# Joining the last 512 rows of a mixture of experts on VectorE, expert by expert, in place of identity products on TensorE

## The chip, the cores and the metric

The kernel runs on one core of one Trainium2 chip. The metric is the device time of one execution in microseconds (us). Three runs of the kernel before gave 262.27, 261.35 and 261.16 us; the median is 261.35 us.

## The reference, cut to what matters

A small language tower over 8 sequences of 256 tokens (2048 rows of 64 channels): a causal convolution tower with log-softmax, a linear attention block, a softmax attention block, and at the end a mixture of 8 experts, top 2 of them weighted. What the change touches is the end of the last stage:

```python
out = zeros_like(flat)                                  # flat: 2048 x 64
for e in range(8):
    hh = silu(flat @ w1[e].T) * (flat @ w3[e].T)        # 2048 x 170
    out = out + weights[:, e:e + 1] * (hh @ w2[e].T)    # 2048 x 64
h = h + x + out
```

Every row needs the sum over the 8 experts of its 64 down-projected values times that row's gate of that expert, plus the row that went in (`hx`, the sum of the residuals).

## The kernel before, in words

The program is written engine by engine, with counting semaphores set and awaited; nothing plans the order, it is the order of the code. Rows lie in 16 tiles of 128 (one row per partition); the last stage takes them in four groups of 512 rows (`PAIRS` = 4, four tiles each). The 170 hidden values of each of the 8 experts make 11 units of up to 128 per group (8 main parts, three packed remainders; `ORDER` says in which order), so the stage has 44 units, u = 0 to 43.

One unit goes through the engines like this: TensorE makes the two up projections into two PSUM banks; ScalarE applies silu (line 746); VectorE multiplies silu by the other projection (line 1229, `hh`); ScalarE rounds the product to float16 (line 731, semaphore `hi_ready`); GpSimd subtracts to get the float16 remainder (`low_part`, line 407, semaphore `lo_ready`). When the parts of a pair of experts k (experts 2k and 2k+1) are there, TensorE makes the down projections of the four tiles (`down(n_, k, t_)`, line 1699), each with three products (high by high, high by low weight, low by high), into one bank of 512 columns: tile, expert of the pair, channel. Even pairs go to bank 6, odd pairs to bank 1. All matmuls have line 1269, that of the helper `mm`.

VectorE then weighs them. `mix` (line 1190) multiplies a whole bank of 128x512 by the gates, broadcast over the channels, and leaves the products in `moe` in SBUF. `mix_add` (line 1197) does an odd pair: it multiplies in place in the bank (line 1201) and adds the bank to the `moe` of the pair before (line 1203). TensorE sums over the pairs and over the two experts of a pair by products with the identity matrix in float32 (`sum_up`, line 1750), into bank 2. `result` (line 1206) adds `hx` and writes the output rows `fin` (the tile `L`). SyncE stores them in eight DMAs of two tiles each (line 263), as `fin_ready` counts up, and at the end waits for all of them (line 264).

The last group (pair index 3, rows of tiles 12 to 15) ends differently. The products of the last pair of experts (k = 3) are made in two parts: `last_high` (line 1728), the 24 matmuls that need only the rounded parts, and `last_low` (line 1741), 12 matmuls that need the remainders of the last unit; tiles 0 and 1 of the group go to bank 1, tiles 2 and 3 to bank 7. Because bank 1 also holds the odd pair k = 1, `last_high` waits for `added`, the end of `mix_add(3, 1)`, which VectorE issues after its last unit (line 1242, i = 10). The identity products are `last_sum(k, i)` (line 1763), for half i of the group: k = 0 ahead of `last_low`, then k = 2 and k = 3 behind it. The code at the end, on TensorE (lines 1836 to 1845):

```python
down(PAIRS - 1, 2, 2)
down(PAIRS - 1, 2, 3)
last_high()
last_sum(0, 0)
last_sum(0, 1)
for t_ in range(4):
    last_low(t_)
for k in (2, 3):
    for i in range(2):
        last_sum(k, i)
```

and on VectorE (lines 1259 to 1263): `mix` of pair 2 (bank 6), `mix` of pair 3 for tiles 0 and 1 (bank 1) and for tiles 2 and 3 (bank 7), then `last_result(0)` and `last_result(1)` (line 1214), which add `hx` to the sums of each half.

The helper `link` makes an instruction signal a semaphore and makes the next one wait for it.

Of the kernel before, what the change touches and what calls it, by code (L numbers as in the profile page):

```python
# [7 lines left out]
B, T, C, V, EMB = 8, 256, 64, 64, 32  # L8
# [5 lines left out]
PAIRS, TILES, P = 4, 16, 128  # L14
RC = 3
CH = NE + RC
# [11 lines left out]
def tower(nc, x, tcn_w, tcn_b, out2_b, emb, in_b, attn_q, attn_e, qkv_w, wo_t, ln1, ln2, router,  # L28
# [8 lines left out]
    with ctx:  # L37
# [3 lines left out]
        def sem(name):  # L41
# [138 lines left out]
                 "rexp_ready", "gate_ready", "a_ps", "b_ps", "sil_ready", "hh_ready", "w2_ps", "mix_ready",  # L180
                 "sum_ps", "added", "fin_ready", "wts_ready", "w1cast", "w2_scaled", "w2_cast", "hx_ready", "hi_ready", "lo_ready",
                 "wt_zero_low", "wt_zero_high"]
# [15 lines left out]
        ROUTE_BANK = ((1, 0), (1, 0), (2, 256), (2, 288))  # L198
        A_BANK, B_BANK, DOWN_BANK, SUM_BANK = (0, 4), (3, 5), (6, 1), 2
        geP = bank[7][:, 0:256].rearrange("p (a i j) -> p a i j", a=4, j=NE)  # L200
# [553 lines left out]
        def _(dve):  # L754
# [451 lines left out]
            def result(n_):  # L1206
# [5 lines left out]
                                 hx[:, g4, :], ALU.add).then_inc(S["fin_ready"], 2)  # L1212

            def last_result(i):

                g2 = slice(TILES - 4 + 2 * i, TILES - 2 + 2 * i)
                dve.wait_ge(S["hx_ready"], PAIRS)
                dve.wait_ge(S["sum_ps"], 2 * PAIRS - 1 + i)
                V_.tensor_tensor(fin[:, g2, :], bank[(SUM_BANK, A_BANK[0])[i]][:, 0:128]
                                 .rearrange("p (t c) -> p t c", c=C), hx[:, g2, :], ALU.add) \  # L1220
                    .then_inc(S["fin_ready"], 1)

            for u in range(PAIRS * CH):
                n_, i = u // CH, u % CH
                dve.wait_ge(S["sil_ready"], u + 1)
                dve.wait_ge(S["b_ps"], u + 1)
# [12 lines left out]
                if i == 7:  # L1239
                    mix(n_, 0, DOWN_BANK[0])  # L1240
                if i == 10:
                    mix_add(n_, 1)
# [9 lines left out]
                for p_, (first, second, third) in enumerate(GATE_STEPS):  # L1252
# [4 lines left out]
                    if u == third:  # L1257
                        gates(p_)
            mix(PAIRS - 1, 2, DOWN_BANK[0])
            mix(PAIRS - 1, 3, DOWN_BANK[1], slice(0, 2))  # L1260
            mix(PAIRS - 1, 3, 7, slice(2, 4))
            last_result(0)
# [4 lines left out]
        def _(pe):  # L1267
            def mm(out_, l_, r_, a, z, skip=False):
                return nc.tensor.matmul(out_, l_, r_, start=a, stop=z, skip_group_check=skip)  # L1269
# [458 lines left out]
            def last_high():  # L1728
                pe.wait_ge(S["hi_ready"], PAIRS * CH)
                pe.wait_ge(S["added"], 2 * PAIRS - 1)  # L1730
                pe.wait_ge(S["gate_ready"], PAIRS)
                for t_ in range(4):
                    c, o = slice(P * t_, P * t_ + P), bank[(DOWN_BANK[1], 7)[t_ // 2]][:, P * t_:P * t_ + P]
                    for w_ in range(2):
                        mm(o, hhx[:, PLACE[NE + 2], 0, c], w2xh[:, w_, NE - 2:NE, :].rearrange("p e c -> p (e c)"),
                           t_ % 2 == 0 and w_ == 0, False)
                        for e in range(2):
                            mm(o[:, C * e:C * e + C], hhx[:, PLACE[NE - 2 + e], 0, c], w2h[:, w_, NE - 2 + e, :], False,
                               False)

            def last_low(t_):
                pe.wait_ge(S["lo_ready"], PAIRS * CH)
                c, o = slice(P * t_, P * t_ + P), bank[(DOWN_BANK[1], 7)[t_ // 2]][:, P * t_:P * t_ + P]
                mm(o, hhx[:, PLACE[NE + 2], 1, c], w2xh[:, 0, NE - 2:NE, :].rearrange("p e c -> p (e c)"), False, False)
                for e in range(2):
                    r = mm(o[:, C * e:C * e + C], hhx[:, PLACE[NE - 2 + e], 1, c], w2h[:, 0, NE - 2 + e, :], False,
                           t_ % 2 == 1 and e == 1)
                r.then_inc(S["w2_ps"], 1)
# [13 lines left out]

            def last_sum(k, i):

                tt = slice(2 * i, 2 * i + 2)
                if k == 0:
                    pe.wait_ge(S["added"], 2 * PAIRS - 1)
                    pe.wait_ge(S["fin_ready"], 2 * PAIRS - 2)
                    pe.wait_ge(S["sil_ready"], PAIRS * CH)
                else:  # L1770
                    pe.wait_ge(S["mix_ready"], 2 * PAIRS + (0 if k == 2 else i + 1))
                for e in range(2):
                    r = mm(bank[(SUM_BANK, A_BANK[0])[i]][:, 0:2 * C].rearrange("p (t c) -> p t c", c=C), identf[:, :],
                           moe[:, k, tt, e, :], k == 0 and e == 0, k == 3 and e == 1)
                if k == 3:
                    r.then_inc(S["sum_ps"], 1)

# [60 lines left out]
            last_high()  # L1838
            last_sum(0, 0)
            last_sum(0, 1)  # L1840
            for t_ in range(4):
                last_low(t_)
            for k in (2, 3):
                for i in range(2):
                    last_sum(k, i)

# [50 lines left out]
```

## Time and profile before

| | us |
|---|---|
| median of 3 runs | 261.35 |
| the profiled execution's own time | 262.08 |
| its span, first to last recorded instruction | 260.4 |
| TensorE busy | 227.3 (87%) |
| VectorE busy | 182.4 (70%) |
| ScalarE busy | 163.3 (63%) |
| GpSimd busy | 148.2 (57%) |
| mean granted TensorE clock | 0.993 of full speed |

Times in the rows are microseconds from the start of the span. PE is TensorE's matmul side, PEld its weight loads, DVE VectorE, ACT ScalarE, POOL GpSimd, SP SyncE; a q behind the name is that engine's sequencer. In a timeline a row is start, duration, engine, line, operation, output<-inputs, count; a row with xN spans N instructions, from the start of the first to the end of the last.

### The profile page before, as it was taken

How to read it: one execution, taken by the hardware profiler on the slowest of the kernel's cores; microseconds unless marked ns; L12 is line 12 of the kernel's file. 1: busy time of each engine (PE TensorE's matmuls, PEld its weight loads, DVE VectorE, ACT ScalarE, POOL GpSimd, SP SyncE). 2: the span in 40 equal slices, each digit the busy share in tenths (PEclk: the TensorE clock that was granted, in tenths of full speed). 3: DMA queues.
4: the chain of work that ended last, by engine and by line, in shares of the span. 5: the costliest groups of instructions: out<-in, count | busy, mean ns of one | idle time of the engine just before them, and what ended most of it. 6: DMA issues, size and time to landing. Idle time of an engine off the chain costs nothing.

```text
span 260.4 us, 6604 instructions
## 1 busy us (share of the span) xinstructions
PE 227.3 (87%) x2457; PEld 156.9 (60%) x2465; DVE 182.4 (70%) x429; ACT 163.3 (63%) x292; POOL 148.2 (57%) x189
## 2 busy tenths in 40 slices
PE   8978779879898999998779878999889989889986
PEld 3645445457576686886556556774456556455665
DVE  4137467842368578688998978957987975999582
ACT  2578753858878578665445435658766578576660
POOL 6997001113366666175073768656798784877780
PEclk9999999979999999999999999999999999999999
DMA  2675200000000000000000000000000010000010
GB/s 37 147 171 137 56 4 1 3 0 0 3 1 0 3 0 4 0 4 0 3 0 3 0 3 1 3 3 0 3 3 3 1 23 3 0 23 0 3 25 20
DMA packets 7467, 4.48 MB, mean 17 GB/s; under 512 B 6500, under 2 KB 6796, under 8 KB 7436
## 3 DMA queue, kind: packets, MB, share of 16 engines
q1 hardware_dynamic: 7436, 4.06, 6.6%
q8 instruction: 20, 0.33, 0.5%
q14 instruction: 11, 0.09, 0.1%
HBM read 3.53 MB, written 0.52 MB: 16 GB/s over the span
## 4 chain that ended last, share of the span: by engine, by line
PE 51%; DVE 26%; ACT 10%; issue 9%; POOL 3%; DVEq 0%; ACTq 0%; POOLq 0%
PE bank L1269 50%; DVE nmx L1046 3%; DVE shared L1229 3%; ACT qT L746 1%; POOL shared L407 1%; ACT qT L616 1%; ACT shared L582 1%; DVE shared L904 1%; DVE early L793 1%; ACT early L507 1%; ACT shared L731 1%; PE bank L1487 1%; ACT shared L596 1%; POOL stat L345 1%; DVE ex L1054 1%
## 5 line engine op out<-in xcount | busy, mean ns | idle before, releaser
L1269 PE MATMUL bank<-early 64*64 64x256 f32 (+4 forms) x561 | 58.2, 352 | 11.6 <-DVE early L793 2.7
L407 POOL TENSOR_TENSOR shared<-shared 128x512 f16<-128x512 f32 x44 | 51.3, 1166 | 16.1 <-ACT shared L731 13.2
L1269 PEld LDWEIGHTS bank<-early 64*64 64x64 f32 (+3 forms) x561 | 31.3, 126 | 30.4 <-issue 5.5
L1229 DVE SCALAR_TENSOR_TENSOR shared<-bank,qT 128x512 f32<-128x512 f32 x44 | 29.7, 688 | 12.7 <-ACT qT L746 12.0
L345 POOL TENSOR_TENSOR stat<-stat,neghalf 128x4 f32<-128x4 f32 x16 | 16.2, 1013 | 36.2 <-DVE stat L878 27.9
L1269 PE MATMUL bank<-qT,shared 128*128 128x256 f32 x112 | 31.8, 396 | 3.8 <-DVE shared L904 3.0
L731 ACT CAST shared<-shared 128x512 f16<-128x512 f32 x44 | 27.0, 614 | 11.6 <-DVE shared L1229 11.6
L746 ACT ACTIVATE qT<-bank 128x512 f32<-128x512 f32 x44 | 26.3, 597 | 10.9 <-PE bank L1269 10.7
L440 POOL TENSOR_TENSOR oTx<-oT,oTx 128x512 f16<-128x512 f32 x16 | 19.1, 1191 | 19.5 <-ACT oTx L628 19.5
L1269 PE MATMUL bank<-onehot,w3h 128*128 128x512 f16 x88 | 26.3, 380 | 2.8 <-DVE shared L1229 2.7
L1269 PE MATMUL bank<-onehot,w1h 128*128 128x512 f16 x88 | 26.2, 379 | 0.3 <-ACT qT L746 0.3
L1269 PEld LDWEIGHTS bank<-qT,shared 128*128 128x128 f32 x112 | 20.9, 195 | 7.8 <-issue 3.9
L1269 PE MATMUL bank<-w2xh,shared 128*128 128x128 f16 (+1 forms) x240 | 22.4, 209 | 3.3 <-POOL shared L407 2.2
L1269 PE MATMUL bank<-w2h,shared 128*128 128x64 f16 x384 | 22.7, 193 | 0.0
L1269 PEld LDWEIGHTS bank<-w2xh,shared 128*128 128x128 f16 x240 | 15.7, 98 | 10.6 <-POOL shared L407 4.3
L904 DVE TENSOR_TENSOR shared<-bank,trimul 128x512 f32<-128x512 f32 x16 | 11.0, 689 | 15.2 <-PE bank L1269 14.9
L682 ACT ACTIVATE qT<-bank 128x512 f32<-128x512 f32 x24 | 14.3, 597 | 8.5 <-PE bank L1269 8.4
L622 ACT ACTIVATE oT<-bank 128x512 f32<-128x512 f32 x16 | 9.6, 598 | 15.2 <-PE bank L1269 15.1
L1269 PE MATMUL bank<-shared 128*128 128x256 f32 x64 | 18.8, 398 | 0.1
L1269 PEld LDWEIGHTS bank<-w2h,shared 128*128 128x128 f16 x384 | 18.3, 98 | 0.0
L793 DVE TENSOR_TENSOR early<-early 128x512 f32<-128x512 f32 x10 | 6.9, 692 | 15.1 <-ACT early L507 14.7
L1046 DVE TENSOR_REDUCE nmx<-bank 128x2 f32<-128x512 f32 (+1 forms) x24 | 15.9, 685 | 2.1 <-PE bank L1269 1.5
(226 smaller groups left out, 481.7 us busy)
## 6 DMA issues: line engine op xcount, KB each, us to landing
early<-in_tcn_w_dram SPq DMA_DIRECT2D x2, 320.0 KB, 4.4
w1s<-in_w1m_dram SPq DMA_DIRECT2D x2, 256.0 KB, 3.7
qT<-in_w3m_dram SPq DMA_DIRECT2D x2, 256.0 KB, 3.4
out_dram<-L SPq DMA_DIRECT2D x8, 64.0 KB, 1.7
qw<-in_attn_q_dram SPq DMA_DIRECT2D x2, 128.0 KB, 2.9
hTs<-in_w2m_dram SPq DMA_DIRECT2D x1, 256.0 KB
cos<-in_cos_t_dram SPq DMA_DIRECT2D x2, 96.0 KB, 2.6
sin<-in_sin_t_dram SPq DMA_DIRECT2D x2, 96.0 KB, 2.3
```

What stands on the lines that cost most here:

```text
L345: nc.gpsimd.tensor_tensor(stat[:, dst, g4], stat[:, src, g4], neghalf[:, 0:4], ALU.pow) \
L407: nc.gpsimd.tensor_tensor(hhx[:, i, 1, :], hh[:, u % RING, :], hhx[:, i, 0, :], ALU.subtract).then_inc(S["lo_ready"], 1)
L440: nc.gpsimd.tensor_tensor(oTx[:, g % 2, 1, :, :], oT[:, g % 2, :, :], oTx[:, g % 2, 0, :, :], ALU.subtract).then_inc(S["o_low"], 1)
L622: nc.scalar.mul(oT[:, g % 2, :, :].rearrange("p a (cc t) -> p cc a t", cc=2), bank[6][:, :].rearrange("p (cc a t) -> p cc a t", cc=2, a=4) ...
L682: nc.scalar.activation(pT[:, b % 2, u, :], bank[5 + (3 * b + u) % 2][:, :], ACT.Exp).then_inc(S["exp2_ready"], 1)
L731: nc.scalar.copy(hhx[:, i, 0, :], hh[:, u % RING, :]).then_inc(S["hi_ready"], 1)
L746: nc.scalar.activation(sil[:, u % 2, :], bank[A_BANK[u % 2]][:, :], ACT.Silu, scale=1.0 / FFN_SCALE).then_inc(S["sil_ready"], 1)
L793: V_.tensor_tensor(x_, x_, hid2[:, 2 * s:2 * s + 2, :], ALU.add).then_inc(S["x_ready"], 1)
L904: V_.tensor_tensor(om[:, g % 2, :].rearrange("p (a t) -> p a t", t=64), bank[4][:, :].rearrange("p (a t) -> p a t", t=64), trimul[:, :].un ...
L1046: V_.tensor_reduce(nmx[:, g, h0:h0 + nh], bank[3 + (3 * b + u) % 2][:, :].rearrange("p (n s) -> p n s", n=nh), AX, ALU.max, negate=True).t ...
L1229: V_.scalar_tensor_tensor(hh[:, u % RING, :], bank[B_BANK[u % 2]][:, :], HH_SCALE / FFN_SCALE, sil[:, u % 2, :], ALU.mult, ALU.mult).then_ ...
L1269: return nc.tensor.matmul(out_, l_, r_, start=a, stop=z, skip_group_check=skip)
```

## The change

The last 512 rows are no longer summed by identity products. VectorE joins them into `fin`. The odd pair k = 1 is weighed in place in bank 1 ahead of the last unit's product instead of behind it (`last_odd`). Behind the last unit, `last_rows_in` adds `moe` of pair 0 to bank 1 (128x512), then adds the first experts' half with `hx` and the second experts' half (128x256 each) into `fin`. `last_even` takes pair 2 straight from bank 6: for each expert and tile one instruction, 128x64, that multiplies by the gate (one value per partition, read from SBUF) and adds `fin`. `last_result(i)` does the same with the last pair, two tiles and two experts. The last pair's products now go to banks 0 and 7, so `last_high` waits for the last silu (`sil_ready`) and no longer for `added`. All `last_sum` are gone. There are three new semaphores.

```diff
+            def last_odd():
+                d_ = downs(DOWN_BANK[1], slice(0, 4))
+                dve.wait_ge(S["w2_ps"], 16 * PAIRS - 8)
+                V_.tensor_tensor(d_, d_, weights_of(PAIRS - 1, 1, slice(0, 4)), ALU.mult).then_inc(S["odd_mixed"], 1)
+
+            def last_rows_in():
+                d_, g4 = downs(DOWN_BANK[1], slice(0, 4)), slice(TILES - 4, TILES)
+                dve.wait_ge(S["odd_mixed"], 1)
+                dve.wait_ge(S["mix_ready"], 2 * PAIRS - 1)
+                link(V_.tensor_tensor(d_, d_, moe[:, 0, :, :, :], ALU.add))
+                dve.wait_ge(S["hx_ready"], PAIRS)
+                link(V_.tensor_tensor(fin[:, g4, :], d_[:, :, 0, :], hx[:, g4, :], ALU.add))
+                V_.tensor_tensor(fin[:, g4, :], d_[:, :, 1, :], fin[:, g4, :], ALU.add).then_inc(S["last_acc"], 4)
+
+            def add_expert(k, e, t_, b_):
+                g, n_ = TILES - 4 + t_, 2 * k + e
+                return V_.scalar_tensor_tensor(fin[:, g, :], downs(b_, slice(t_, t_ + 1))[:, 0, e, :],
+                                               gate[:, g, n_:n_ + 1], fin[:, g, :], ALU.mult, ALU.add)
+
+            def last_even():
+                dve.wait_ge(S["w2_ps"], 16 * PAIRS - 4)
+                dve.wait_ge(S["last_acc"], 4)
+                for e in range(2):
+                    for t_ in range(4):
+                        if e:
+                            dve.wait_ge(S["last_acc"], 5 + t_)
+                        add_expert(2, e, t_, DOWN_BANK[0]).then_inc(S["last_acc"], 1)
+
             def last_result(i):
-                g2 = slice(TILES - 4 + 2 * i, TILES - 2 + 2 * i)
-                dve.wait_ge(S["hx_ready"], PAIRS)
-                dve.wait_ge(S["sum_ps"], 2 * PAIRS - 1 + i)
-                V_.tensor_tensor(fin[:, g2, :], bank[(SUM_BANK, A_BANK[0])[i]][:, 0:128]
-                                 .rearrange("p (t c) -> p t c", c=C), hx[:, g2, :], ALU.add) \
-                    .then_inc(S["fin_ready"], 1)
+                first, second = 2 * i, 2 * i + 1
+                dve.wait_ge(S["w2_ps"], 16 * PAIRS - 2 + 2 * i)
+                dve.wait_ge(S["last_acc"], 12)
+                add_expert(3, 0, first, LAST_BANK[i]).then_inc(S["last_odd"], 1)
+                add_expert(3, 0, second, LAST_BANK[i]).then_inc(S["last_odd"], 1)
+                dve.wait_ge(S["last_odd"], 3 * i + 1)
+                add_expert(3, 1, first, LAST_BANK[i]).then_inc(S["last_odd"], 1)
+                dve.wait_ge(S["last_odd"], 3 * i + 3)
+                add_expert(3, 1, second, LAST_BANK[i]).then_inc(S["fin_ready"], 1)
 
             for u in range(PAIRS * CH):
                 n_, i = u // CH, u % CH
+                if u == PAIRS * CH - 1:
+                    last_odd()
...
-                if i == 10:
+                if i == 10 and n_ < PAIRS - 1:
                     mix_add(n_, 1)
...
-            mix(PAIRS - 1, 2, DOWN_BANK[0])
-            mix(PAIRS - 1, 3, DOWN_BANK[1], slice(0, 2))
-            mix(PAIRS - 1, 3, 7, slice(2, 4))
+            last_rows_in()
+            last_even()
             last_result(0)
             last_result(1)
...
             def last_high():
                 pe.wait_ge(S["hi_ready"], PAIRS * CH)
-                pe.wait_ge(S["added"], 2 * PAIRS - 1)
+                pe.wait_ge(S["sil_ready"], PAIRS * CH)
                 pe.wait_ge(S["gate_ready"], PAIRS)
                 for t_ in range(4):
-                    c, o = slice(P * t_, P * t_ + P), bank[(DOWN_BANK[1], 7)[t_ // 2]][:, P * t_:P * t_ + P]
+                    c, o = slice(P * t_, P * t_ + P), bank[LAST_BANK[t_ // 2]][:, P * t_:P * t_ + P]
...
             last_high()
-            last_sum(0, 0)
-            last_sum(0, 1)
             for t_ in range(4):
                 last_low(t_)
-            for k in (2, 3):
-                for i in range(2):
-                    last_sum(k, i)
```

`LAST_BANK` is (0, 7), and `last_low` writes there too.

## Rows read from the trace of the kernel before

**Rows 1.** The head of the page, span and busy time of the engines

```profile
span 260.4 us, 6604 instructions
PE 227.3 (87%) x2457; PEld 156.9 (60%) x2465; DVE 182.4 (70%) x429; ACT 163.3 (63%) x292; POOL 148.2 (57%) x189
```

**Rows 2.** The chain that ended last, in order of time, from 250.7 us: start, us, what

```profile
250.71 0.61 ACT qT L746
...
251.34 0.70 DVE shared L1229
...
252.07 0.63 ACT shared L731
...
253.47 4.38 PE bank L1269 x60
...
257.94 0.29 DVE L L1219
```

**Rows 3.** Timeline of TensorE's matmuls, 249.9 us to the end

```profile
249.99 0.25 PE L1269 MATMUL bank<-w2h,shared 128*128 128x64 f16 x3
...
252.14 0.34 PE L1269 MATMUL bank<-w2h,shared 128*128 128x64 f16 x6
253.47 0.22 PE L1269 MATMUL bank<-w2xh,shared 128*128 128x128 f16 x1 [0.99 <-ACT shared L731]
...
254.32 0.22 PE L1269 MATMUL bank<-w2h,shared 128*128 128x64 f16 x2
254.38 1.14 PE L1269 MATMUL bank<-qst,identf 128*128 128x128 f32 x8
255.35 0.22 PE L1269 MATMUL bank<-w2xh,shared 128*128 128x128 f16 x1
...
255.52 0.22 PE L1269 MATMUL bank<-w2h,shared 128*128 128x64 f16 x2
...
255.75 0.22 PE L1269 MATMUL bank<-w2h,shared 128*128 128x64 f16 x2
255.81 2.03 PE L1269 MATMUL bank<-qst,identf 128*128 128x128 f32 x16
```

**Rows 4.** Timeline of VectorE, 249.8 us to the end

```profile
249.78 0.69 DVE L1229 SCALAR_TENSOR_TENSOR shared<-bank,qT 128x512 f32<-128x512 f32 x1 [0.21 <-ACT qT L746]
251.34 0.69 DVE L1229 SCALAR_TENSOR_TENSOR shared<-bank,qT 128x512 f32<-128x512 f32 x1 [0.87 <-ACT qT L746]
251.95 0.69 DVE L1201 TENSOR_TENSOR bank<-bank,gate 128x512 f32<-128x512 f32 x1
252.68 0.69 DVE L1203 TENSOR_TENSOR qst<-bank,qst 128x512 f32<-128x512 f32 x1
253.28 0.68 DVE L1194 TENSOR_TENSOR qst<-bank,gate 128x512 f32<-128x512 f32 x1
255.85 0.76 DVE L1194 TENSOR_TENSOR qst<-bank,gate 128x256 f32<-128x256 f32 x2 [1.89 <-PE bank L1269]
257.50 0.29 DVE L1219 TENSOR_TENSOR L<-bank,hx 128x128 f32<-128x128 f32 x1 [0.89 <-PE bank L1269]
257.94 0.29 DVE L1219 TENSOR_TENSOR L<-bank,hx 128x128 f32<-128x128 f32 x1 [0.15 <-PE bank L1269]
```

**Rows 5.** Timeline of GpSimd, its last two instructions

```profile
251.95 2.40 POOL L407 TENSOR_TENSOR shared<-shared 128x512 f16<-128x512 f32 x2 [0.35 <-ACT shared L731]
```

**Rows 6.** Groups of VectorE's instructions by line and shape: busy us, mean ns

```profile
L1211 DVE TENSOR_TENSOR L<-bank,hx 128x256 f32<-128x256 f32 x3 | 1.2, 414 | 0.0
...
L1138 DVE SCALAR_TENSOR_TENSOR gate<-gate,bank 128x32 f32<-128x32 f32 x4 | 0.7, 187 | 0.1
...
L809 DVE SCALAR_TENSOR_TENSOR qkvh<-qkvw,lns,qkvh 128x128 f16<-128x128 f32 x1 | 0.4, 352 | 0.0
...
L809 DVE SCALAR_TENSOR_TENSOR rwh<-rw,lns,rwh 128x8 f16<-128x8 f32 x1 | 0.2, 227 | 0.0
```

**Rows 7.** Line 785: min/median/max ns of one, and its timeline row

```profile
L785 DVE TENSOR_SCALAR onehot<-bank,vcol x4: 472/473/482, 5.8 to 7.0; 128x255 f32<-128x255 f32 x4
...
5.83 1.65 DVE L785 TENSOR_SCALAR onehot<-bank,vcol 128x255 f32<-128x255 f32 x4
```

**Rows 8.** SyncE's last two stores, and the time from issue to landing

```profile
257.82 0.89 SPq L263 DMA_DIRECT2D out_dram<-L  x2
...
DMA to landing us min/median/max: 1.6/1.7/1.7
```

More of the change, by code:

```diff
@@ L180, in tower @@
                  "rexp_ready", "gate_ready", "a_ps", "b_ps", "sil_ready", "hh_ready", "w2_ps", "mix_ready",
-                 "sum_ps", "added", "fin_ready", "wts_ready", "w1cast", "w2_scaled", "w2_cast", "hx_ready", "hi_ready", "lo_ready",
+                 "sum_ps", "added", "odd_mixed", "last_acc", "last_odd", "fin_ready", "wts_ready", "w1cast", "w2_scaled", "w2_cast", "hx_ready", "hi_ready", "lo_ready",
                  "wt_zero_low", "wt_zero_high"]
@@ L198, in tower @@
         ROUTE_BANK = ((1, 0), (1, 0), (2, 256), (2, 288))
-        A_BANK, B_BANK, DOWN_BANK, SUM_BANK = (0, 4), (3, 5), (6, 1), 2
+        A_BANK, B_BANK, DOWN_BANK, SUM_BANK, LAST_BANK = (0, 4), (3, 5), (6, 1), 2, (0, 7)
         geP = bank[7][:, 0:256].rearrange("p (a i j) -> p a i j", a=4, j=NE)
@@ L1742, in last_low @@
                 pe.wait_ge(S["lo_ready"], PAIRS * CH)
-                c, o = slice(P * t_, P * t_ + P), bank[(DOWN_BANK[1], 7)[t_ // 2]][:, P * t_:P * t_ + P]
+                c, o = slice(P * t_, P * t_ + P), bank[LAST_BANK[t_ // 2]][:, P * t_:P * t_ + P]
                 mm(o, hhx[:, PLACE[NE + 2], 1, c], w2xh[:, 0, NE - 2:NE, :].rearrange("p e c -> p (e c)"), False, False)
@@ L1761, in sum_up @@
                 r.then_inc(S["sum_ps"], 1)
[L1763 to L1776, printed above, removed]
             for u in range(PAIRS * CH):
```

## The prediction

> **What bounds the kernel now.** The page's head comes first: TensorE is busy 87% of the span [rows 1], but the change leaves the first 43 of 44 units alone, so that share doesn't price it. The chain of waits is read next, at its end [rows 2]: the last silu, VectorE's product, ScalarE's rounding, then TensorE alone from 253.47 to 257.85, and one small addition of VectorE. So the last 4.4 us are a TensorE tail. What it consists of is in the matmul timeline [rows 3]: `last_high` from 253.47, identity products (8 records) at 254.38, `last_low` from 255.35, and 16 more identity records from 255.81. The VectorE timeline [rows 4] shows the other side: it idles 1.89 us before the last pair's weighing and 0.89 us before the first result. Last comes what the remaining work can't be earlier than: GpSimd's two last remainders end at 251.95 + 2.40 = 254.35 [rows 5], and `last_low` needs them. Today it starts 1.0 us after that, behind the identity products of pair 0.
>
> The end to beat is 257.94 + 0.29 = 258.23, when the last `fin` rows stand [rows 4]. Behind it come the issue of the last store and its landing (1.7 us) [rows 8]; the span ends 2.2 us behind the last rows, and that part stays.
>
> **Part 1: the odd pair's weighing ahead of the last product.** `last_odd` needs `down(3, 1, 3)`, whose last matmul ends at 249.99 + 0.25 = 250.24 [rows 3]. VectorE is on unit 42 from 249.78 and can start the next free instruction 0.61 us later: that is the distance between 251.34 and 251.95, two instructions without a wait on each other, though each lasts 0.69 [rows 4]. So it runs from 250.39 to 251.08, within the 0.87 us that VectorE spends waiting for silu before 251.34. Cost nothing; without that cover it would delay the last product, and all behind it, by up to 0.61 us. What is queued behind it is only that product, which has 0.26 us in hand.
>
> **Part 2: rows in.** The last product starts at 251.34 as before. `last_rows_in` follows at 251.95 with a 128x512 addition from PSUM and SBUF (0.69, as line 1203). Each of the next two waits for the one before: from 251.95 + 0.69 to 252.68 is 0.04 [rows 4]. They are 128x256 with a PSUM source, 0.414 each, as line 1211 [rows 6]. So: 251.95 + 0.69 + 0.04 + 0.41 + 0.04 + 0.41 + 0.04 = 253.59, the start of `last_even`. Its products in bank 6 end at 252.14 + 0.34 = 252.48 [rows 3], so it doesn't wait for them. Removed here are line 1203, and the three `mix` (0.68, and 0.76 for the two together).
>
> **Part 3: TensorE.** `last_high` no longer waits for `added`, only for the rounding that ends at 252.07 + 0.63 = 252.70 [rows 2]; it starts near 252.75 instead of 253.47 and takes 0.9 (253.47 to 254.38), to 253.65 [rows 3]. Then nothing stands before `last_low`, and it starts as the remainders land: 254.40. Before, VectorE could read tiles 0 and 1 half a microsecond after `last_low` began (255.35 to 255.85) [rows 3, 4]; so they are ready at 254.90 and tiles 2 and 3 some 0.23 later (255.52 to 255.75). All 24 float32 identity records go; none of them is replaced on TensorE. The last silu reads bank 4, not bank 0, and ended at 251.31, so the new bank costs no wait.
>
> **Part 4: the sixteen small adds, the term that decides.** They are 128x64 `scalar_tensor_tensor` with a per-partition scalar read from SBUF, a PSUM source and `fin`. The trace has no such shape. The nearest rows are the same operation with such a scalar, 352 ns for 128 columns and 227 for 8 [rows 6]: 1.04 ns per column, so 285 ns for 64. A second way: line 785, a per-partition scalar and a PSUM source, 473 ns at 255 columns [rows 7], less 191 columns at 1.04, gives 274. From below: the form without such a scalar is 187 ns at 32 columns [rows 6], so 220 at 64; from above: no more than the 352 of the double width.
>
> The distance from start to start matters more than the duration. Line 785 has four in a row, 1.65 us from the first start to the last end: (1.65 - 0.473)/3 = 0.392, again 0.08 less than one lasts. So I take 285 ns each and 0.205 apart where no wait holds them, and 0.285 + 0.04 where one must see the end of the one before.
>
> `last_even`: in its second half each add waits for the one four places earlier, long done; so 7 x 0.205 + 0.285 + 0.04 = 1.76 until `last_result(0)`, at 255.35. That is behind 254.90: VectorE, not TensorE, is late next. `last_result`: two free adds, a third whose partner is done by then, and a fourth that waits for the third: it starts at 2 x 0.205 + 0.325 = 0.735. The second call follows 0.205 later, at 0.94, and ends at 0.94 + 0.735 + 0.285 = 1.96. So the last rows stand at 255.35 + 1.96 = 257.31, the first half's at 256.37.
>
> The first store is then issued 0.94 us ahead of the second, instead of 0.44, and the two issues together took 0.89 [rows 8]; so the second finds SyncE free. It may have lost 0.04 to that before, which I leave out.
>
> **The sum.** 257.31 against 258.23: 0.92 us earlier. The profiled execution took 262.08 with a span of 260.4, so 261.2 and 259.5 after. The median of the runs, 261.35, is 0.73 below the profiled one; taking 0.92 from it gives 260.43. In terms of the distance p between adds the tail is 16p + 0.44 (a duration being p + 0.08), and 4.64 us (253.59 to 258.23) are there for it. A change of 10 ns in p is 0.16 us. The bounds: p = 0.14 from the form without the scalar gives 2.7, a gain of 1.9; line 785's p = 0.193 gives a gain of 1.1; p = 0.27 from the 352 ns gives 4.8, a loss of 0.1.
>
> On the distance: line 785 and the pairs of 128x512 [rows 4, 7] start 0.08 before the one in front has ended. The Trainium skill, "VectorE: DVE Perf Modes", section "The DRAIN you can't avoid", says that the next operation does not start until the pipeline is empty, unless its instruction isn't held; taken as it stands this would put every add 0.285 us or more behind the last, and the tail would be the slower rival's below. The overlaps in the rows speak against it here.
>
> **Rivals.** (a) *The scalar costs nothing once the instructions overlap.* The 128x512 pair starts 0.61 apart, that is 0.53 for the columns at 1.04 and 0.077 fixed [rows 4]; 64 columns would be 0.143 apart. Tail 16 x 0.143 + 0.44 = 2.73, and then `last_result(0)` would wait 0.1 for TensorE: gain 1.8, time 259.5. Against it: line 785 keeps a fixed part of 0.392 - 0.266 = 0.126 between starts. The Trainium skill's "Vector Engine (DVE) Microarchitecture Reference", section "Measured stream behaviour on trn2", gives about 75 ns per instruction after overlap for built-in operations; that is this rival's figure.
>
> (b) *The adds run one behind the other.* Place: `last_even` and `last_result`, where every add counts a semaphore up and half of them stand behind a wait, and the instructions are short. Each would cost 0.285 + 0.04 = 0.325 and the tail 16 x 0.325 = 5.2: 0.5 us slower than before, 261.9; with 352 ns each, 6.3, 1.6 us slower, 263.0. It decides from 0.29 us per add (4.64/16) on. For it: no row shows instructions of 64 columns with a scalar in front of each other and a wait between. Against it: the pairs of 0.61 in [rows 4] have waits that are already met between them, and they overlap.
>
> (c) *TensorE stays late.* If `last_low` began at its old time, `last_result(0)` would start at 255.85, the last rows stand at 257.81: gain 0.4, time 260.9. Against it: nothing is left in its queue between `last_high` and the remainders.
>
> (d) *The change does less than it says*: `last_odd` falls on the path and takes back 0.3 to 0.6 us; 260.8 to 261.0.
>
> **How the numbers follow.** Forecast 0.60; (a) 0.16; (b) 0.12; (c) and (d) 0.06 each. The predicted time is the forecast's, 260.4. The low end is (a) with 0.2 for scatter, 259.3; the high end takes in the first case of (b), 262.0, and leaves out its worse one. A difference of under 0.5%, 1.3 us, is about what can't be told from none in a measurement of this kernel. Faster by more needs p below 0.18: (a), and a small part of the forecast, since it lies 0.4 us short: 0.22. Slower by more needs 0.37 us per add: the worse end of (b) and what I have not seen, 0.05. Within 0.5%: 0.73.
>
> **What would show it.** In the profile after: `last_odd` between 250.4 and 251.1 and the last product still at 251.34; `last_low` within 0.1 us of GpSimd's end; the 128x64 adds at 285 ns, 0.205 apart in the run of eight; no idle time of VectorE behind the last product that TensorE ends; last rows at 257.3. The forecast is wrong if the eight adds of `last_even` take over 2.3 us or under 1.3, or if VectorE waits for `w2_ps` in the tail.

## The result: 1.1 us faster, as forecast

Fifteen runs of each kernel, taken in turn: 260.90 us (260.09 to 261.77) against 262.05 (261.16 to 262.72) for the kernel before. The ratio is 0.9958, with a 95% interval of 0.9946 to 0.9970: 0.8 to 1.4 us faster, 1.1 in the middle. Forecast were 0.92 us, a time of 260.4 within 259.3 to 262.0, and a chance of 0.73 for a difference under 0.5%. The profiled execution took 261.01 us, its span is 259.3.

The page's head after, against [rows 1]:

```profile
span 259.3 us, 6567 instructions
PE 224.5 (87%) x2433; PEld 154.4 (60%) x2441; DVE 184.8 (71%) x442; ACT 163.2 (63%) x292; POOL 148.1 (57%) x189
```

TensorE has 24 matmul records fewer (2457 to 2433), the identity products. VectorE has 13 instructions more and is busy 2.4 us longer. The engine that got more work is the one that now ends sooner, which only the end of the trace explains. The timeline of VectorE after, which answers to [rows 4] (columns as there):

```profile
249.67 0.69 DVE L1266 SCALAR_TENSOR_TENSOR shared<-bank,qT 128x512 f32<-128x512 f32 x1 [0.21 <-ACT qT L746]
250.28 0.69 DVE L1218 TENSOR_TENSOR bank<-bank,gate 128x512 f32<-128x512 f32 x1
251.23 0.69 DVE L1266 SCALAR_TENSOR_TENSOR shared<-bank,qT 128x512 f32<-128x512 f32 x1 [0.27 <-ACT qT L746]
251.84 0.69 DVE L1225 TENSOR_TENSOR bank<-bank,qst 128x512 f32<-128x512 f32 x1
252.56 0.42 DVE L1227 TENSOR_TENSOR L<-bank,hx 128x256 f32<-128x256 f32 x1
253.09 0.42 DVE L1228 TENSOR_TENSOR L<-bank,L 128x256 f32<-128x256 f32 x1
253.63 3.61 DVE L1233 SCALAR_TENSOR_TENSOR L<-bank,gate,L 128x64 f32<-128x64 f32 x16
```

The long idle times of [rows 4] (1.89 and 0.89 us, both ended by TensorE) are gone; behind the last product VectorE works without a stop that another engine ends. The odd pair's weighing (line 1218) lies in the gap before the last product. The last rows stand at 253.63 + 3.61 = 257.24.

TensorE and GpSimd after, answering to [rows 3] and [rows 5], from their timelines: the first matmul of `last_high`, the first of `last_low`, and GpSimd's last two:

```profile
252.63 0.23 PE L1305 MATMUL bank<-w2xh,shared 128*128 128x128 f16 x1 [0.27 <-ACT shared L731]
...
254.29 0.23 PE L1305 MATMUL bank<-w2xh,shared 128*128 128x128 f16 x1 [0.57 <-POOL shared L407]
```

```profile
251.84 2.40 POOL L407 TENSOR_TENSOR shared<-shared 128x512 f16<-128x512 f32 x2 [0.36 <-ACT shared L731]
```

`last_low` starts 0.05 us behind the end of the remainders (254.24), where it used to start 1.0 behind.

**How to compare two traces here.** The last product of VectorE starts at 251.34 before and at 251.23 after, though nothing ahead of it changed but one instruction in a gap. Across the twelve kernels run below, which share that part but for the same instruction, it starts anywhere from 250.28 to 251.85. So spans, and single times, carry up to 1.5 us that are not the change's. What the change does is read from the **tail**: from the start of the last product to the end of the last addition into `fin`. Before, 258.23 - 251.34 = 6.89 us; after, 257.24 - 251.23 = 6.01. That is 0.88 us less.

Behind the last rows come 2.17 us before (260.4 - 258.23) and 2.06 after (259.3 - 257.24).

### The profile page after: what moved, and what is told of

Read it like the earlier page. It is cut to its first block, busy times and chain, and to the rows that moved or that the text cites. A ratio compares the mean times of both kernels' runs of the same rounds, so it can differ in the third digit from the quotient of the medians.

```text
span 259.3 us, 6567 instructions
## 1 busy us (share of the span) xinstructions
PE 224.5 (87%) x2433; PEld 154.4 (60%) x2441; DVE 184.8 (71%) x442; ACT 163.2 (63%) x292; POOL 148.1 (57%) x189
## 4 chain that ended last, share of the span: by engine, by line
PE 50%; DVE 27%; ACT 10%; issue 8%; POOL 3%; DVEq 0%; ACTq 0%; POOLq 0%
PE bank L1305 48%; DVE nmx L1046 3%; DVE shared L1266 2%; ACT qT L746 1%; POOL shared L407 1%; DVE L L1233 1%; ACT qT L616 1%; DVE early L793 1%; ACT early L507 1%; DVE shared L904 1%; PE bank L1523 1%; DVE s L896 1%; ACT shared L596 1%; POOL stat L345 1%; DVE s L1090 1%
## 5 line engine op out<-in xcount | busy, mean ns | idle before, releaser
L1305 PE MATMUL bank<-early 64*64 64x256 f32 (+4 forms) x561 | 58.9, 354 | 11.3 <-DVE early L793 2.7
L1305 PE MATMUL bank<-qT,shared 128*128 128x256 f32 x112 | 31.2, 388 | 3.9 <-DVE shared L904 3.0
L1305 PEld LDWEIGHTS bank<-qT,shared 128*128 128x128 f32 x112 | 20.2, 190 | 8.0 <-issue 4.4
L1305 PE MATMUL bank<-shared 128*128 128x256 f32 x64 | 17.8, 380 | 0.1
```

## The experiments

The tails, each from its own VectorE timeline, beside the times (ratio to the kernel before on the same chip, 95% interval):

| kernel | last product starts | last rows | tail | ratio (interval) |
|---|---|---|---|---|
| before | 251.34 | 258.23 | 6.89 | 1 |
| after | 251.23 | 257.24 | 6.01 | 0.9958 (0.9946 to 0.9970) |
| e12_after, the same again | 251.07 | 257.08 | 6.01 | 0.9966 (0.9951 to 0.9982) |
| e1_idle_products | 250.28 | 256.29 | 6.01 | 0.9968 (0.9953 to 0.9983) |
| e11_idle_16 | 251.53 | 258.04 | 6.51 | 0.9986 (0.9968 to 1.0004) |
| e3_old_banks | 251.17 | 257.18 | 6.01 | 0.9982 (0.9971 to 0.9994) |
| e2_odd_behind | 250.75 | 257.49 | 6.74 | 0.9993 (0.9977 to 1.0010) |
| e4_chained | 250.75 | 258.43 | 7.68 | 1.0016 (0.9996 to 1.0037) |
| e5_wide_even | 251.33 | 257.41 | 6.08 | 0.9976 (0.9957 to 0.9996) |
| e6_order_only | 250.33 | 257.17 | 6.84 | 0.9997 (0.9984 to 1.0009) |
| e7_fewer_waits | 250.56 | 256.32 | 5.76 | 0.9940 (0.9919 to 0.9960) |
| e8_scalar_even | 251.85 | 257.65 | 5.80 | 0.9959 (0.9941 to 0.9978) |
| e9_scalar_in_bank | 250.47 | 256.53 | 6.06 | 0.9972 (0.9956 to 0.9989) |
| e10_scalar_shares | 251.29 | 256.61 | 5.32 | 0.9937 (0.9917 to 0.9956) |

The unchanged kernel run twice gives the same tail to 0.01 us, so tenths of a microsecond can be read there. Each tail is from one trace. The ratios can't tell neighbours in the table apart (the intervals are 0.6 to 1.1 us wide), but their order follows the tails nearly throughout. A ratio on record is not the quotient of the two medians. Theory: VectorE's own instructions set the end, at about 0.2 us per small add. Rivals: TensorE's last products set it; the gain came from the waits and the order, not from the identity products; the adds' width or their distance doesn't matter.

### Does TensorE still matter? e1, e11 and e3

```diff
             last_high()
+            pe.wait_ge(S["mix_ready"], 2 * PAIRS - 1)
+            pe.wait_ge(S["fin_ready"], 2 * PAIRS - 2)
+            for i in range(2):                      # e11: (0, 1, 0, 1)
+                for e in range(2):
+                    mm(bank[(SUM_BANK, A_BANK[1])[i]][:, 0:2 * C]..., identf[:, :],
+                       moe[:, 0, 2 * i:2 * i + 2, e, :], e == 0, e == 1)
             for t_ in range(4):
                 last_low(t_)
```

> The changed kernel with the 8 identity records of pair 0 put back between last_high and last_low, into two free banks, their result read by nobody. If VectorE sets the end of the tail: last_high ends near 253.55, the 8 records take 1.0, last_low starts near 254.55 instead of 254.29, tiles 0 and 1 can be read at 255.05, still ahead of 255.36, so the stretch from the start of the last product to the last rows stays at 6.0 us and the time is that of the changed kernel within 0.1 us. If TensorE's last products set the end: 0.25 us longer, 6.26.

> As e1_idle_products with 16 idle identity records ahead of last_low instead of 8. e1 cost nothing; here TensorE's delay is larger than the slack of about 0.5 us: last_low starts 1.95 us behind the end of last_high, 4.3 behind the start of the last product, tiles 0 and 1 can be read at 4.8, where VectorE would take them at 4.13. If VectorE sets the end up to there: the stretch is 0.6 to 0.7 us longer, 6.6 to 6.7.

TensorE's timeline, e1 and then e11: the idle products and the first matmul of `last_low`; below them VectorE's timeline of e11 at the last eight adds.

```profile
252.60 1.14 PE L1305 MATMUL bank<-qst,identf 128*128 128x128 f32 x8
253.57 0.22 PE L1305 MATMUL bank<-w2xh,shared 128*128 128x128 f16 x1
```

```profile
253.85 2.03 PE L1305 MATMUL bank<-qst,identf 128*128 128x128 f32 x16
255.72 0.22 PE L1305 MATMUL bank<-w2xh,shared 128*128 128x128 f16 x1
```

```profile
256.15 1.89 DVE L1233 SCALAR_TENSOR_TENSOR L<-bank,gate,L 128x64 f32<-128x64 f32 x8 [0.59 <-PE bank L1305]
```

Eight idle records cost nothing: 6.01. Sixteen cost 0.50; `last_low` starts 4.19 us behind the last product (255.72 - 251.53), VectorE waits and takes its result 0.43 later. I had expected 0.6 to 0.7, because I put `last_low` at 4.3 and the hand-over at 0.5. With 0.43 for it, the slack in the changed kernel is 255.36 - (254.29 + 0.43) = 0.64 us. Up to there VectorE sets the end; TensorE doesn't.

```diff
-        A_BANK, ..., LAST_BANK = (0, 4), ..., (0, 7)
+        A_BANK, ..., LAST_BANK = (0, 4), ..., (1, 7)
...
-                pe.wait_ge(S["sil_ready"], PAIRS * CH)
+                pe.wait_ge(S["last_acc"], 4)
```

> The changed kernel with the last pair's products back in banks 1 and 7, so that last_high waits until VectorE has read bank 1 (253.5 us). If VectorE sets the end: last_high runs 253.6 to 254.5, last_low right behind, tiles 0 and 1 can be read at 255.0, ahead of 255.36, and the time doesn't change (6.0 us, within 0.1). If the other bank is what brings the gain: last_low and all behind it later by 0.25 us or more.

TensorE's timeline, the first matmul of `last_high`:

```profile
253.55 0.22 PE L1305 MATMUL bank<-w2xh,shared 128*128 128x128 f16 x1 [1.25 <-issue]
```

`last_high` starts 2.38 us behind the last product instead of 1.40, and `last_low` right behind it. Tail 6.01, unchanged. In the changed kernel the move to another bank brings nothing: it earns slack that VectorE doesn't use. What it would bring in the kernel before is another question, taken up with e6.

### The odd pair ahead of the last product: e2

```diff
-                if u == PAIRS * CH - 1:
-                    last_odd()
...
+            last_odd()
             last_rows_in()
```

> The changed kernel with the odd pair's weighing (last_odd) put back behind the last product. If VectorE sets the end: the weighing costs its full 0.61 to 0.73 us, the stretch from the last product to the last rows grows from 6.0 to 6.6 or 6.7 us, and of the gain over the kernel before of about 1.0 us 0.3 is left. If the gain comes from TensorE (identity products gone), it stays at 6.0.

```profile
250.75 0.69 DVE L1264 SCALAR_TENSOR_TENSOR shared<-bank,qT 128x512 f32<-128x512 f32 x1 [0.87 <-ACT qT L746]
251.36 0.69 DVE L1218 TENSOR_TENSOR bank<-bank,gate 128x512 f32<-128x512 f32 x1
...
253.88 3.61 DVE L1233 SCALAR_TENSOR_TENSOR L<-bank,gate,L 128x64 f32<-128x64 f32 x16
```

In VectorE's timeline the 0.87 us gap is back ahead of the product, and the weighing lies behind it. Tail 6.74, 0.73 more: 0.69 and the 0.04 of a wait, since the addition behind it now has to see its end. So 0.73 of the change's 0.88 us of tail hang on this one instruction having been moved into a gap, once VectorE sets the end. In the kernel before TensorE sets it, and no run moved the instruction alone there.

### Is the distance of the adds what counts? e4 and e7

```diff
-                        if e:
-                            dve.wait_ge(S["last_acc"], 5 + t_)
+                        dve.wait_ge(S["last_acc"], 4 + 4 * e + t_)
```

and in the same way in `last_result`: every add waits for the one before.

> The changed kernel with every one of the sixteen 128x64 adds waiting for the end of the one before. If the gain hangs on their overlap: each costs 0.277 + 0.04 to 0.10 us, sixteen take 5.1 to 6.0 us instead of 3.61, and the kernel is 0.5 to 1.4 us slower than the kernel before. If the adds' distance is set by something else than the wait (they are issue-bound): under 0.5 us more than the changed kernel.

Groups by line and shape of e4 in the tail (busy us, mean ns | idle before), and its timeline row:

```profile
L1233 DVE SCALAR_TENSOR_TENSOR L<-bank,gate,L 128x64 f32<-128x64 f32 x16 | 4.5, 284 | 0.8
```

```profile
253.18 5.25 DVE L1233 SCALAR_TENSOR_TENSOR L<-bank,gate,L 128x64 f32<-128x64 f32 x16
```

Sixteen adds take 5.25 us instead of 3.61, the tail is 7.68: slower than the kernel before by 0.79 us in the tail, and in the times by nothing that can be told from zero (1.0016, 0.9996 to 1.0037). This is rival (b) of the prediction, made on purpose. What the chip does with adds that needn't wait is in the changed kernel's row of the line (ns: min/median/max):

```profile
L1233 DVE SCALAR_TENSOR_TENSOR L<-bank,gate,L x16: 274/275/284, 253.6 to 257.0; 128x64 f32<-128x64 f32 x16
```

and in its chain of waits:

```profile
253.63 1.64 DVE L L1233 x8
...
255.36 0.68 DVE L L1233 x3
256.04 0.03 issue
256.06 0.03 DVE L L1233
256.10 0.17 issue
256.26 0.67 DVE L L1233 x3
...
256.96 0.28 DVE L L1233
```

Eight in a row take 1.64 us: (1.64 - 0.275)/7 = 0.195 from start to start. Behind each run of three the chain stops, for the fourth add waits for the third: it starts at 256.06, 0.03 us behind the third's end at 256.04, where the others start 0.08 ahead of it. The fifth then starts 0.20 behind the fourth, at the usual distance. e7 takes the wait away:

```diff
-                dve.wait_ge(S["last_odd"], 3 * i + 1)
-                add_expert(3, 1, first, LAST_BANK[i]).then_inc(S["last_odd"], 1)
-                dve.wait_ge(S["last_odd"], 3 * i + 3)
+                dve.wait_ge(S["last_odd"], 2 * i + 1)
+                add_expert(3, 1, first, LAST_BANK[i]).then_inc(S["fin_ready"], 1)
+                dve.wait_ge(S["last_odd"], 2 * i + 2)
                 add_expert(3, 1, second, LAST_BANK[i]).then_inc(S["fin_ready"], 1)
```

(the last two stores wait for 8 and 10 of `fin_ready`.)

> The changed kernel with the fourth add of each half no longer waiting for the third (the two adds of a half's second expert both count fin_ready up). If the adds' distance of 0.195 us holds there too: the gaps of 0.12 us ahead of the fourth add and of 0.09 behind it go, 0.2 to 0.3 us less in the tail. If the semaphore instructions set the distance: nothing.

```profile
252.97 3.35 DVE L1233 SCALAR_TENSOR_TENSOR L<-bank,gate,L 128x64 f32<-128x64 f32 x16
```

The sixteen now take 3.35 us in VectorE's timeline, the tail is 5.76: 0.25 us for two waits. Its ratio, 0.9940, is below that of the changed kernel, but the intervals overlap; the tail is what parts the two.

### Narrow or wide? e5

```diff
-                for e in range(2):
-                    for t_ in range(4):
-                        ...
-                        add_expert(2, e, t_, DOWN_BANK[0]).then_inc(S["last_acc"], 1)
+                link(V_.tensor_tensor(d_, d_, weights_of(PAIRS - 1, 2, slice(0, 4)), ALU.mult))
+                link(V_.tensor_tensor(fin[:, g4, :], d_[:, :, 0, :], fin[:, g4, :], ALU.add))
+                V_.tensor_tensor(fin[:, g4, :], d_[:, :, 1, :], fin[:, g4, :], ALU.add).then_inc(S["last_acc"], 8)
```

> The changed kernel with pair 2 joined in three wide instructions (128x512 times the gates in place, two 128x256 adds) instead of eight of 128x64. By the rows: 0.69 + 0.04 + 0.42 + 0.04 + 0.42 + 0.09 = 1.70 us against 1.73 (253.63 to 255.36): the same time within 0.1 us. If going expert by expert is itself what brings the gain: 0.5 us or more slower.

```profile
253.72 0.70 DVE L1241 TENSOR_TENSOR bank<-bank,gate 128x512 f32<-128x512 f32 x1
254.46 0.42 DVE L1242 TENSOR_TENSOR L<-bank,L 128x256 f32<-128x256 f32 x1
254.98 0.42 DVE L1243 TENSOR_TENSOR L<-bank,L 128x256 f32<-128x256 f32 x1
255.53 1.88 DVE L1233 SCALAR_TENSOR_TENSOR L<-bank,gate,L 128x64 f32<-128x64 f32 x8
```

From 253.72 to 255.53 VectorE's timeline has 1.81 us for the three wide ones, against 1.73 for the eight narrow ones (253.63 to 255.36). Tail 6.08. Expert by expert is 0.07 us better, no more. At 1.04 ns per column, an estimate from [rows 6], the narrow ones pass 512 columns (0.53 us) and the rest of their time is eight fixed costs of 0.13 and the hand-over at the end; the wide ones pass 1024 columns (1.07) and have 0.74 for three fixed costs and the waits between them.

### Was it the order, in the kernel before? e6

```diff
             last_high()
-            last_sum(0, 0)
-            last_sum(0, 1)
             for t_ in range(4):
                 last_low(t_)
+            last_sum(0, 0)
+            last_sum(0, 1)
```

on the kernel before, with the last pair in banks 0 and 7 and without the wait for `added`.

> The kernel before with only the banks and the order changed: the last pair in banks 0 and 7, last_high without the wait for the odd pair, all 24 identity records behind last_low. If the identity products themselves are the tail's length: last_low starts at 254.4, the 24 records take 2.9 us from 254.8, end at 257.7 to 257.8 against 257.85 before, a gain of 0.0 to 0.2 us. If the waits and the order were the cost: a gain of 0.7 us or more, as last_low starts 1.0 us earlier.

TensorE's timeline, the start of `last_low` and the identity products:

```profile
253.38 0.23 PE L1270 MATMUL bank<-w2xh,shared 128*128 128x128 f16 x1 [0.57 <-POOL shared L408]
...
253.85 2.92 PE L1270 MATMUL bank<-qst,identf 128*128 128x128 f32 x24
```

`last_low` starts 3.05 us behind the last product (253.38 - 250.33) instead of 4.01, and the tail is 6.84 instead of 6.89. In e6 TensorE sets the end: the 24 records follow `last_low` without a stop for 2.92 us, and the last addition starts 0.11 behind them.

But this run changes two things at once. It frees `last_high` from the wait for `added`, and it takes the eight records of pair 0 away from the place where they would have filled TensorE's wait for GpSimd (the 0.57 us in the row above) and puts them behind `last_low`. What the freed wait alone is worth it doesn't show. The rows give an estimate. e1 has the order of the kernel before with `last_high` freed, and its `last_low` starts 253.57 - 250.28 = 3.29 us behind the last product. The sums of pair 0 that the eight records read stand at 252.68 + 0.69 - 251.34 = 2.03 [rows 4], ahead of the 2.32 where the records start in e1. From the start of `last_low` to the last rows the kernel before takes 258.23 - 255.35 = 2.88 [rows 3, 4]. Together that is a tail of 6.17: 0.72 us less than before, with every identity product kept. No run tried this kernel (the last pair in banks 0 and 7, the order as it was). So the rival that the waits were most of the cost isn't refuted. What the runs show is that VectorE's chain, and no longer TensorE's, ends the changed kernel at 6.01; they don't show that the identity products had to go for most of the gain.

### Can the idle engine help? e8, e9 and e10

ScalarE is idle from 252.58 on. e8 lets it weigh pair 2:

```diff
+            for e in range(2):
+                for t_ in range(4):
+                    g = TILES - 4 + t_
+                    nc.scalar.mul(moe[:, 2, t_, e, :], d6[:, t_, e, :], gate[:, g, 4 + e:5 + e]) \
+                        .then_inc(S["act_even"], 1)
...
+                dve.wait_ge(S["act_even"], 4)
+                link(V_.tensor_tensor(fin[:, g4, :], moe[:, 2, :, 0, :], fin[:, g4, :], ALU.add))
+                dve.wait_ge(S["act_even"], 8)
+                V_.tensor_tensor(fin[:, g4, :], moe[:, 2, :, 1, :], fin[:, g4, :], ALU.add).then_inc(S["last_acc"], 8)
```

> The changed kernel with pair 2 weighed by ScalarE, idle after 252.58, in eight 128x64 multiplications into SBUF, and VectorE adding them in two 128x256 instructions. If VectorE sets the end and ScalarE is quick (about 0.12 us apart, done by 253.9): VectorE needs 0.92 instead of 1.64 us, then waits for TensorE until 254.8, so the tail shrinks by 0.55 us to 5.5. If ScalarE needs 0.3 us each, it ends at 255.0 and the gain is 0.1 or less.

Timelines of VectorE, of GpSimd and of ScalarE in e8:

```profile
254.23 0.91 DVE L1250 TENSOR_TENSOR L<-qst,L 128x256 f32<-128x256 f32 x1
255.23 0.43 DVE L1252 TENSOR_TENSOR L<-qst,L 128x256 f32<-128x256 f32 x1
```

```profile
252.46 2.40 POOL L407 TENSOR_TENSOR shared<-shared 128x512 f16<-128x512 f32 x2 [0.35 <-ACT shared L731]
```

```profile
253.11 1.75 ACT L758 ACTIVATE qst<-bank,gate 128x64 f32<-128x64 f32 x8
```

The tail is 5.80, 0.21 less instead of 0.55. ScalarE is not quick: eight take 1.75 us, 0.2 apart. And two additions of one shape, `moe` and `fin`, both in SBUF, take 0.91 and 0.43: the slow one starts while GpSimd runs (until 254.86), the quick one behind it. e9 differs by where VectorE reads:

```diff
-                    nc.scalar.mul(moe[:, 2, t_, e, :], d6[:, t_, e, :], gate[:, g, 4 + e:5 + e]) \
+                    nc.scalar.mul(d6[:, t_, e, :], d6[:, t_, e, :], gate[:, g, 4 + e:5 + e]) \
...
-                dve.wait_ge(S["act_even"], 4)
+                dve.wait_ge(S["act_even"], 8)
```

and both additions read bank 6.

> As e8_scalar_even, but ScalarE writes its products back into bank 6 and VectorE adds from there once all eight are done. Open from e8: its first 128x256 add, SBUF with SBUF, took 0.91 us while GpSimd was running. If GpSimd beside two SBUF sources is the cause: both adds now take 0.42, from about 3.1 us behind the start of the last product (ScalarE's eight end 3.0 behind it), and the stretch to the last rows is 6.0 to 6.1 us (the wait for ScalarE eats what the adds give). If the add is slow because ScalarE writes beside it: 0.42 too, so this run doesn't part those two; if it is slow by its operands' layout: 0.9 again.

```profile
253.56 0.42 DVE L1249 TENSOR_TENSOR L<-bank,L 128x256 f32<-128x256 f32 x1 [0.81 <-ACT bank L757]
```

0.42 us, but it had to start 0.09 us behind GpSimd's end (251.08 + 2.39 = 253.47), as ScalarE had not been done before. So e9 doesn't show the bank to be quick beside GpSimd; the changed kernel does: its additions of bank and `L` or `hx` (lines 1227 and 1228) lie at 252.56 and 253.09, in the middle of GpSimd's 251.84 to 254.24, and take 0.42. In e8 ScalarE was writing too while the slow one ran. The kernel before parts the two. Three stretches of its timeline: ScalarE alone beside additions of SBUF with SBUF; an addition of line 926, also SBUF with SBUF, with GpSimd beside it; and line 926 again with ScalarE and no GpSimd beside it:

```profile
28.14 1.53 DVE L793 TENSOR_TENSOR early<-early 128x512 f32<-128x512 f32 x2 [1.85 <-ACT early L507]
28.25 0.69 ACT L507 ACTIVATE early<-bank,bt 128x512 f32<-128x512 f32 x1 [0.20 <-PE bank L1269]
28.84 0.62 ACT L543 ACTIVATE w2h<-hTs 128x512 f16<-128x512 f32 x1
```

```profile
80.85 1.16 POOL L440 TENSOR_TENSOR oTx<-oT,oTx 128x512 f16<-128x512 f32 x1
80.98 1.30 DVE L926 TENSOR_TENSOR xf<-qw,stat 128x256 f32<-128x256 f32 x1 [0.32 <-POOL stat L345]
```

```profile
141.94 0.41 DVE L926 TENSOR_TENSOR xf<-qw,stat 128x256 f32<-128x256 f32 x1
141.99 0.80 ACT L637 COPY early<-bank 96x768 bf16<-96x768 bf16 x1
```

All ten of line 793 take 0.691 to 0.693, the two here with ScalarE writing beside them: it doesn't slow them. Line 926 runs four times. Three start just behind the start of GpSimd's line 440 and take 1.30, 1.37 and 1.37; each ends 0.27 or 0.28 behind GpSimd's end (here 82.28 against 82.01), as the slow addition of e8 does (255.14 against 254.86). The fourth has no GpSimd beside it and takes 0.41. So GpSimd beside two SBUF sources is the cause, by these rows.

The Trainium skill, "SBUF — State Buffer", section "Who interferes with whom", says that a VectorE instruction with two SBUF inputs contends with a GpSimd instruction that reads SBUF, through a shared read interface, and that one with at most one SBUF input, outside the two-port modes, doesn't. The rows of the kernel before, of the changed kernel and of e8 agree.

e10 uses both findings. ScalarE weighs only the second expert of pair 2 (before VectorE comes to bank 6) and the last pair's tiles 2 and 3; VectorE adds these wide, after GpSimd's end; and e7's wait is gone:

```diff
...
+            for t_ in range(4):
+                g = TILES - 4 + t_
+                nc.scalar.mul(moe[:, 2, t_, 1, :], d6[:, t_, 1, :], gate[:, g, 5:6]) \
+                    .then_inc(S["act_even"], 1)
+            act.wait_ge(S["w2_ps"], 16 * PAIRS)
...
+            for e in range(2):
+                for t_ in (2, 3):
+                    g = TILES - 4 + t_
+                    nc.scalar.mul(moe[:, 3, t_, e, :], d7[:, t_, e, :], gate[:, g, 6 + e:7 + e]) \
+                        .then_inc(S["act_last"], 1)
...
```

> A version meant to beat both kernels. ScalarE weighs the second expert of pair 2 (four 128x64, 0.2 us apart, done before VectorE gets to bank 6) and the last pair's tiles 2 and 3 (bank 7) into SBUF; VectorE adds these wide, behind GpSimd's end; and the fourth add of the first half doesn't wait for the third. If VectorE's work sets the end: 5.4 us from the last product to the last rows, against 6.0 of the changed kernel and 6.9 of before: 1.5 us faster than before (0.994 or 0.995), 0.6 faster than the changed kernel. If ScalarE's part comes late or the hand-overs cost more than 0.1 us each: 5.8 or more.

```profile
253.68 0.86 DVE L1247 SCALAR_TENSOR_TENSOR L<-bank,gate,L 128x64 f32<-128x64 f32 x4
254.64 0.43 DVE L1259 TENSOR_TENSOR L<-qst,L 128x256 f32<-128x256 f32 x1
255.17 0.86 DVE L1247 SCALAR_TENSOR_TENSOR L<-bank,gate,L 128x64 f32<-128x64 f32 x4
255.95 0.28 DVE L1267 TENSOR_TENSOR L<-qst,L 128x128 f32<-128x128 f32 x1
256.32 0.29 DVE L1269 TENSOR_TENSOR L<-qst,L 128x128 f32<-128x128 f32 x1
```

In VectorE's timeline eight narrow adds are left of sixteen, and three wide ones stand for the other eight. Tail 5.32, 0.69 less than the changed kernel and 1.57 less than before. Times: 260.19 us median against 260.96 of the changed kernel on the same chip and 261.49 of the kernel before; the ratio to before is 0.9937 (0.9917 to 0.9956). It has the shortest tail of all and is faster than before by more than the interval; against the changed kernel (0.9966, 0.9951 to 0.9982) the intervals just overlap, and the tails decide.

> The changed kernel itself, unchanged, beside the others on the same chip: 6.01 us from the start of the last product to the last rows, a ratio of 0.996 to the kernel before.

Tail 6.01, ratio 0.9966: as expected, to a tenth of a percent.

## Why the prediction was right

**Part 1** held: `last_odd` at 250.28, 0.61 behind unit 42's product, the last product not delayed (its gap 0.27 instead of 0.87). e2 shows what it is worth: 0.73 us.

**Part 2** was 0.15 us short. I had 2.25 us from the last product to `last_even`; it was 253.63 - 251.23 = 2.40. Between lines 1227 and 1228 lie 0.11 us, not 0.04, and 0.12 between 1228 and the first add. In the chain of waits a sequencer step of VectorE stands in both places, and none between 1225 and 1227, which are 0.03 apart. Why is open. It isn't the number of waits in the code: in e5 line 1242 waits for 1241 and line 1243 for 1242, each only through `link`, and the gaps are 0.04 (254.42 to 254.46) and 0.10 (254.88 to 254.98).

**Part 3** held: `last_high` 1.40 us behind the last product (1.41 forecast), `last_low` 3.06 (3.06), and not waited for. e1 and e11 give the slack, 0.64 us; I had 0.45.

**Part 4**, the deciding term: 275 ns and 0.195 apart measured, 285 and 0.205 taken; both nearer to line 785's way (274 and 0.193) than to the one I chose. Sixteen took 3.61 us instead of 3.72. My reason for the other row was that the operation is the same; the row with a PSUM source and the same kind of scalar was the nearer one. e4 confirms the formula's other end: chained, they are 0.32 apart (0.284 and 0.04), where I had 0.325.

**The sum**: tail 6.01 measured, 257.31 - 251.34 = 5.97 forecast. The 0.15 too little in part 2 and the 0.11 too much in part 4 cancel to within 0.04. That is luck: each part by itself was off by 0.11 or more. Of the measured 1.1 us (0.8 to 1.4), 0.88 are the tail's. Behind the last rows the profiled execution has 0.11 less (2.17 to 2.06 us). SyncE's timeline, the last store's issue, before (from 258.2 us) and then after (from 257.3 us):

```profile
258.26 0.44 SPq L263 DMA_DIRECT2D out_dram<-L  x1
```

```profile
257.27 0.37 SPq L263 DMA_DIRECT2D out_dram<-L  x1
```

It starts 0.03 us behind the last rows in both, so the 0.04 that I thought the first store might cost it was not there; it is 0.07 shorter, and why is not shown. The changed kernels' other traces end 2.0 to 2.1 behind the last rows too. The rest of the 1.1 is within the scatter.

**The rivals**: (a) no: the per-partition scalar keeps its cost between starts, 0.195 and not 0.143. The Trainium skill's figure of about 75 ns per instruction after overlap ("Vector Engine (DVE) Microarchitecture Reference", "Measured stream behaviour on trn2") fits the 128x512 pair of [rows 4] (0.077), not these: 0.195 less 64 columns at 1.04 leaves 0.128. (b) no, and e4 shows what it would have been: 0.8 us slower in the tail, not to be told from no change in the times. My first price for it, 0.5, was 0.3 short, and mostly not in the adds: sixteen took 5.25 us where I had 5.20, but they started 253.18 - 250.75 = 2.43 behind the last product instead of 2.25, part 2's error again. The Trainium skill's "VectorE: DVE Perf Modes", section "The DRAIN you can't avoid", also says that a next operation that isn't held starts earlier. The rows agree with that exception, 0.195 from start to start at 0.275 each; my prediction left it aside when it put every add 0.285 us behind the last. (c) no: `last_low` came with GpSimd. (d) no.

The prediction is right on what it forecast: which engine ends the tail, and when. It says nothing of how much the freed wait of `last_high` would have brought with the identity products kept; by the estimate under e6 that is 0.7 us, and it stays untested. Open too is the difference between the measured 1.1 us and the 0.9 to 1.0 that the tail and what follows it explain; the interval holds both.

## What to carry to other kernels

A chain of waits that ends on one engine for microseconds asks two questions: which of its work has to be there, and what the other engine could do in its idle time. Here 24 records of float32 identity products (2.9 us) were traded for sixteen small VectorE instructions (3.6 us), and it paid because VectorE had been idle for 2.9 of the last 4.3 us and one 0.7 us instruction fitted a gap further ahead. Before trading, ask what a wait in the chain is worth by itself: here `last_high` stood 0.7 us behind its inputs for the sake of a bank, and lifting that wait alone was never tried. Where small instructions follow each other, their start-to-start distance (0.195 us) is the price, and each wait for the one just before adds 0.12 us: order them so that none waits for its neighbour. And measure such a change by the stretch it touches (repeatable to 0.01 us here), not by spans that differ by 1.5 us for reasons ahead of it.

## What the runs showed of the hardware that I had not expected

- An addition of 128x256 with both sources in SBUF took 0.91 us where it began beside GpSimd's subtraction, and 0.43 behind its end; with one source in PSUM it took 0.42 beside GpSimd. The slow ones ended 0.27 to 0.28 behind GpSimd's end.
- ScalarE is no quicker than VectorE at 128x64 from PSUM with a per-partition scale: 0.31 to 0.36 us each into SBUF, and 0.2 us apart (e8, eight in 1.75 us), though its 128x512 instructions take 0.6.
- A VectorE instruction that waits for the one in front started 0.03 to 0.04 us behind its end in some pairs and 0.10 to 0.11 in others, though the code has one wait in both (e5, lines 1242 and 1243).
- Waiting for the one in front cost a 128x64 add 0.12 us from start to start (0.32 against 0.195), though nothing but the wait was different.
